# Causal attention's first batch: half of the query stores and loads, and the first maxima, sent by ScalarE

## What is computed

```
x = x + causal_attention(layernorm(x))    # 32 query heads of 16, one key and value head, ALiBi bias
x = x + ffn(layernorm(x))
x = x + window_attention(layernorm(x))
x = x + ffn(layernorm(x))
```

```
qkv    = hidden_states @ Wqkv                       # q: 32 heads x 16, k and v: 16 each
scores = einsum('bqhd,bkd->bhqk', q, k) * d**-0.5   # plus the ALiBi slope, minus 1e30 above the diagonal
probs  = softmax(scores)
attn   = einsum('bhqk,bkd->bqhd', probs, v)
out    = attn.reshape(B, S, H) @ Wo
```

## Time and profile before

| what | value |
|---|---|
| median of 3 runs | 2748.94 us |
| lowest and highest | 2740.22 and 2750.15 us |
| the profiled execution, own time | 2754.62 us |
| its span in the trace | 2752.8 us |
| its mean granted TensorE clock | 0.965 |
| first `scores` of batch 0 start at | 83.25 us |

### The profile page before, as it was taken

One profiled execution on the slowest core, in us unless ns is written; L12 is line 12 of the kernel. 1 busy time (PEld: TensorE's weight loads), 2 busy tenths in 40 slices (PEclk: granted clock), 3 DMA queues, 4 the chain that ended last, 5 costly groups with the idle time before them and its releaser, 6 DMA issues. The chain is left out here.

```text
span 2752.8 us, 41641 instructions
## 1 busy us (share of the span) xinstructions
PE 2590.5 (94%) x14444; PEld 2024.3 (74%) x14444; DVE 1731.8 (63%) x3500; ACT 1308.5 (48%) x2952; POOL 1018.4 (37%) x890
## 2 busy tenths in 40 slices
PE   4789998899999799999999998999999999799998
PEld 2445444477778588888888876888888888577777
DVE  3575656178777556565666656665666666587775
ACT  2354546332222366656666645666665666232221
POOL 2112122173333344344444423445444443443322
PEclk7889999899999999999999999999999999899999
DMA  4335242310000210011100110111001100300000
GB/s 150 111 90 139 66 114 62 85 74 1 1 0 1 64 31 16 31 38 38 38 30 8 39 39 1 39 39 38 30 8 38 38 23 1 120 1 16 16 15 16
DMA packets 113464, 117.43 MB, mean 43 GB/s; under 512 B 6244, under 2 KB 85988, under 8 KB 113316
## 3 DMA queue, kind: packets, MB, share of 16 engines
q1 hardware_dynamic: 112448, 115.51, 13.8%
q10 hardware_dynamic: 900, 0.40, 0.1%
HBM read 92.09 MB, written 22.68 MB: 42 GB/s over the span
## 5 line engine op out<-in xcount | busy, mean ns | idle before, releaser
L2024 POOL TENSOR_TENSOR rope_straight<-rope_straight,rope_crossed 128x512 f32<-128x512 f32 x160 | 207.1, 1294 | 526.8 <-DVE rope_crossed L1808 526.8
L599 POOL TENSOR_TENSOR f_hidden_low<-f_hidden,f_hidden_high 128x256 fp32r<-128x256 f32 x224 | 186.3, 852 | 427.8 <-ACT f_hidden_high L539 427.6
L1826 DVE TENSOR_TENSOR o_low<-o_sum,o_high 128x512 fp32r<-128x512 f32 x128 | 88.5, 692 | 316.5 <-ACT o_high L2004 316.2
L1035 DVE TENSOR_REDUCE a_max<-a_work 128x1 f32<-128x384 f32 (+3 forms) x352 | 205.5, 635 | 110.8 <-PE a_work L923 108.7
L1918 ACT ACTIVATE probs<-probs,exp_bias 128x256 f32<-128x256 f32 (+1 forms) x512 | 240.2, 471 | 3.3 <-DVE exp_bias L1791 3.2
L1160 ACT ACTIVATE a_probs<-a_scores 128x512 f32<-128x512 f32 x320 | 173.9, 597 | 141.2 <-PE a_scores L937 70.7
L1929 ACT CAST q_high<-rope_straight 128x512 fp32r<-128x512 f32 x128 | 79.5, 621 | 298.4 <-POOL rope_straight L2024 298.4
L1923 ACT ACTIVATE probs<-probs,exp_sum_inverse 128x256 f32<-128x256 f32 (+1 forms) x512 | 205.1, 471 | 32.4 <-DVE exp_sum_inverse L1796 32.4
L539 ACT CAST f_hidden_high<-f_hidden 128x512 fp32r<-128x512 f32 x112 | 69.5, 620 | 314.2 <-PE f_acc L296 159.8
L1628 PE MATMUL w_sum<-o_high,wo_high 128*128 128x512 f32 x512 | 204.9, 400 | 8.7 <-DVE xt L1833 4.8
L1628 PE MATMUL w_sum<-o_high,wo_low 128*128 128x512 f32 x512 | 204.2, 399 | 0.0
(11 more groups left out here) (241 smaller groups left out, 7435.9 us busy)
## 6 DMA issues: line engine op xcount, KB each, us to landing
a_queries<-a_q_stacked SPq DMA_DIRECT2D x16, 1024.0 KB, 6.1
wq_raw<-in_L_attn_b_wq SPq DMA_DIRECT2D x32, 512.0 KB, 3.7
wo_raw<-in_L_attn_b_wo SPq DMA_DIRECT2D x16, 1024.0 KB, 6.5
a_q_stacked<-a_q_part_high SPq DMA_DIRECT2D x32, 256.0 KB
f_w_raw<-in_L_ffn_w SPq DMA_DIRECT2D x14, 512.0 KB, 10.5
f_w_raw<-in_L_ffn_w2t SPq DMA_DIRECT2D x14, 512.0 KB, 11.3
a_q_stacked<-a_q_part_low SPq DMA_DIRECT2D x16, 256.0 KB
wkv_raw<-in_L_attn_b_wk SPq DMA_DIRECT2D x16, 256.0 KB, 6.5
```

The source lines that it names most:

```text
L599: e.tensor_tensor(hl[:, j % 2, cols], hm[:, cols], f32(hh[:, j % 2, cols]), ALU.subtract).then_inc(hl_ready, 1)
L1035: e.tensor_reduce(mx[:, t % 2, to:to + nh], bank, AX.X, ALU.max).then_inc(work_free[k], 1)
L2024: e.tensor_tensor(ra[:, slot], ra[:, slot], rb[:, slot], ALU.add).then_inc(roped, 1)
```

## The change

Four functions that issue DMAs move out of SyncE's program, get the engine `e` as an argument, and are called by ScalarE too. In batch 0 ScalarE now issues the query stores of m = 1 (after its cast of m = 2) and of m = 3 (after its cast of m = 3), the query loads of tiles 1 and 3 (after the squares of batch 1) and the maxima of tile 0. SyncE keeps the stores of m = 0 and 2 and the loads of tiles 0 and 2. The loads of `wo_raw` and of batch 2's `x` move behind the maxima of tile 1. Later batches are as before.

```
+        def send_queries(e, b, m):
+            if m == 0:
+                for t in range(ST):
+                    wait(e, q_landed[t], 16 * b)
+            e.wait_ge(q_low, b * DT + m + 1)
+            half, head = divmod(8 * m, HEADS)
+            for row, part in ((R_QHI, qsh), (R_QLO, qsl), (R_QHI2, qsh)):
+                to = q_dram[half, row:row + AD, head:head + 8, :].rearrange("d h t -> h d t")
+                e.dma_start(to, f32(part[:, m % 2])).then_inc(q_stored[m % 2], 16)
+
+        def load_queries(e, b, t):
+            if b:
+                e.wait_ge(scores_full, (b - 1) * UNITS_A + 4 * (t + 1) * (t + 2))
+            e.dma_start(f32(qa[:, :, t * P:(t + 1) * P]),
+                        q_dram[:, :, :, t * P:(t + 1) * P].rearrange("a r h t -> (a r) h t")).then_inc(q_landed[t], 16)
...
         @block.scalar
...
                     e.copy(qsh[:, i % 2], bank[:, :]).then_inc(q_high, 1)
+                    if b == 0 and i >= 2:
+                        e.wait_ge(q_rows_in, 32)
+                        send_queries(e, 0, 2 * i - 3)
                 elif kind == "mT":
                     e.wait_ge(full, n)
                     wait(e, m_landed[i % 2], 32 * (b * 2 + i // 2))
                     e.activation(mh[:, i % 2], bank[0:AH, 0:P], ACT.Copy, scale=-1.0).then_inc(m_high, 1)
+                    if b == 0 and i == 0:
+                        send_max(e, 0, 0)
...
                     if step == ["mean", 1, 0]:
                         for d in range(DT):
                             square(1, d)
+                        queries_stored(e, 0)
+                        e.wait_ge(masks_ready, 3)
+                        for t in (1, 3):
+                            load_queries(e, 0, t)
...
         @block.sync
...
             e.wait_ge(q_rows_in, 32)
-            for m in range(DT):
-                send_queries(0, m)
-            queries_stored(0)
+            for m in (0, 2):
+                send_queries(e, 0, m)
+            queries_stored(e, 0)
             e.wait_ge(masks_ready, 3)
-            for t in range(ST):
-                load_queries(0, t)
-            e.dma_start(wo_raw[:, :, :], wo.rearrange("(t p) n -> p t n", p=P)).then_inc(wo_in, 16)
-            send_max(0, 0)
-            load_x(2)
+            for t in (0, 2):
+                load_queries(e, 0, t)
...
                 if b == 0:
-                    send_max(0, 1)
+                    send_max(e, 0, 1)
+                    e.dma_start(wo_raw[:, :, :], wo.rearrange("(t p) n -> p t n", p=P)).then_inc(wo_in, 16)
+                    load_x(2)
```

More of the change, by code:

```diff
@@ L846, in load_last, with queries_stored, send_max @@
                     .then_inc(out_landed[m], 16)
+        def send_queries(e, b, m):
[12 more added lines that the diff above has]
+                        q_dram[:, :, :, t * P:(t + 1) * P].rearrange("a r h t -> (a r) h t")).then_inc(q_landed[t], 16)
+        def queries_stored(e, b):
+            for k in range(2):
+                e.wait_ge(q_stored[k], 48 * DT // 2 * (b + 1))
+        def send_max(e, b, t):
+            par = t % 2
+            e.wait_ge(m_low, b * ST + t + 1)
+            for row, part in ((R_MAX, mh), (R_MAX + 1, ml)):
+                e.dma_start(f32(qa[row:row + 65:64, :, t * P:(t + 1) * P]), f32(part[:, par, :])).then_inc(m_landed[par], 16)
         block = st.enter_context(nc.Block())
@@ L1303, in send_keys @@
                         e.dma_start(f32(keys[b % 2][r:r + AD, :]), f32(part[32:KV, :])).then_inc(k_landed, 16)
-            def send_queries(b, m):
-                if m == 0:
-                    for t in range(ST):
[L1308 to L1329, removed]
             def load_sums(b):
@@ L1388, in _ @@
                 if b == 0:
-                    send_max(0, 1)
+                    send_max(e, 0, 1)
+                    e.dma_start(wo_raw[:, :, :], wo.rearrange("(t p) n -> p t n", p=P)).then_inc(wo_in, 16)
+                    load_x(2)
                 if more:
-                    send_queries(b + 1, 0)
-                    send_queries(b + 1, 1)
+                    send_queries(e, b + 1, 0)
+                    send_queries(e, b + 1, 1)
                 if b:
-                    send_max(b, 2)
+                    send_max(e, b, 2)
                     store_inverses(b - 1)
@@ L1398, in _ @@
                 if more:
-                    send_queries(b + 1, 2)
+                    send_queries(e, b + 1, 2)
                 if b == 0:
-                    send_max(0, 2)
+                    send_max(e, 0, 2)
                 if more:
[L1403 to L1406, removed]
+                    send_queries(e, b + 1, 3)
+                    queries_stored(e, b + 1)
+                    load_queries(e, b + 1, 0)
+                    load_queries(e, b + 1, 1)
                 for qt in range(2):
@@ L1409, in _ @@
                         store_out(e, b, qt, half)
-                send_max(b, 3)
+                send_max(e, b, 3)
                 if b == 0:
@@ L1413, in _ @@
                 if more:
-                    load_queries(b + 1, 2)
+                    load_queries(e, b + 1, 2)
                 for half in range(2):
@@ L1417, in _ @@
                 if more:
-                    send_max(b + 1, 0)
-                    send_max(b + 1, 1)
-                    load_queries(b + 1, 3)
+                    send_max(e, b + 1, 0)
+                    send_max(e, b + 1, 1)
+                    load_queries(e, b + 1, 3)
             e.wait_ge(inv_ready, NB)
```

## The result

The changed kernel takes 2751.85 us (median of 20 runs, 2745.38 to 2760.87), the kernel before 2745.91 us in the 20 runs beside it (one of these took 6270 us; without it the median is 2745.69). The ratio is 1.0020 with a 95% interval of 1.0012 to 1.0029, which is 3.3 to 8.0 us slower. The forecast was 5.3 us slower and 2754, with 2745 to 2761 as its range.

The account below looks back on a forecast made before the run. The prediction took TensorE, busy 94% of the span, as the bound, so only its first `scores` mattered: layernorm +8.7 us, maxima ready 8.8 late, their wait -3.4, in all +5.3 on the median 2748.94, giving 2754, range 2745 to 2761.

Parts of the forecast that it names:

- What bounds the start: Before TensorE's first `scores`, the layernorm of batch 1 (70.39 us), not the load (68.57), is the last thing the maxima await.
- Stores of m = 1, +7.9 us: ScalarE issues them only behind its cast of m = 2, so its cast of m = 3 comes at 60.0, not 52.13.
- Half of the engines: Query stores use half of the DMA engines, fully; the two queues' stores share the same eight, at a share of 0.5.
- the rival of two queues beside each other: ScalarE's stores meet free DMA engines, m = 1 lands at 55.7, +1.0 us in all, 2750; chance 0.12.
- Stores of m = 3: Issued by ScalarE from 61.35 us, landed at 68.2 instead of 62.53, +5.7 us.
- ScalarE's issues ahead of the squares, +0.8 us: ScalarE issues DMAs until 63.1 though batch 1's squares could begin at 62.3, making the layernorm +8.7 us.
- ScalarE's issue of the loads: Two loads on ScalarE take 2.46 us from 68.2, end before the seed is wanted at 72.1, and cost nothing.
- The rival: The loads block ScalarE for 3.4 and 3.54 us, +3.0 on the layernorm, +8.3 in all; chance 0.14.
- Tile 0 shared with tile 1: Loads from two queues each get half the rate, so tile 0 is there at 77.8 us, level with VectorE's 79.1.
- Maxima, -3.4 us: TensorE's wait for tile 0's maxima falls from 6.1 to 2.7 us through the moves of `wo_raw` and the maxima.
- Sum: First `scores` start at 88.6 us against 83.25, +5.3 us.
- The shift reaches the end: From the first `scores` on, every engine follows TensorE, so a shift of that start passes to the end one for one.

Follow-up runs that it names:

- stores only: The kernel before with only the query stores of m = 1 and m = 3 moved to ScalarE; ratio to before 1.0024, median 2753.23 us.
- with 16 engines: The kernel before with Wqkv's query columns ordered (feature, head), so a store's slowest dimension is 16, not 8; ratios to before 0.9978 and, run again, 0.9970.
- loads only: The kernel before with only the query loads of tiles 1 and 3 moved to ScalarE; ratio to before 0.9994.
- changed, 16 engines: The changed kernel with Wqkv's query columns ordered (feature, head), slowest store dimension 16; ratios to the kernel before 0.9978 and, run again, 0.9985.
- weights behind only: The kernel before with only `wo_raw` and batch 2's `x` moved behind the maxima of tile 1; ratio to before 0.9992, median 2745.01 us.

## Why the prediction was right

*What bounds the start.* Right. In every kernel VectorE goes from the layernorm of batch 1 to its first maximum with no gap of over 0.1 us, and in "stores only" and with 16 engines TensorE is seen waiting for it.

*Stores of m = 1, +7.9 us.* It measured +6.0 (58.17 for 52.13), just below the 59 to 61 us that I gave as a sign of being right. The mechanism was right: the store stands behind a cast that waits for other stores. I let ScalarE issue at 48.9, when its cast has ended, and it issued at 47.61, which is 1.3 us less. Of these, 0.7 us are m = 0, which landed that much earlier. The rest is that the issue came 0.08 us after the cast began and not after its end; all that these stores wait for, the low part of m = 1, had been ready since 43.1. The other 0.5 us lie in the six stores themselves, 10.6 us from issue to use for 11.1. With m = 1 put back behind its own cast, the same kernel is 5.6 us faster to the `scores`.

*Half of the engines.* Shown as a share: 0.51 with one queue or two, 0.89 with a slowest dimension of 16. So the rival of two queues beside each other was out. One remark of the prediction was not quite right: SyncE was held up a little by issuing stores before, its fifth took 1.64 us (from 43.97) where the first took 0.66. Nothing waited for it.

*Stores of m = 3.* 59.56 to 66.43 is 6.9 us, the forecast's 61.35 to 68.2 as well.

*ScalarE's issues ahead of the squares, +0.8 us.* It measured 1.1: the squares start 1.84 us after VectorE's mean, 0.72 before. The layernorm came out at +7.1 (77.52 for 70.39), with 8.7 forecast.

*ScalarE's issue of the loads.* Costs nothing in the changed kernel: they end at 70.20 and the seed starts at 70.45. I had written 2.46 us for them and left 1.4 us of room; they took 3.76 and 0.25 was left. In "loads only" the cover is gone, and the seed is 2.7 us late. The rival was nearer than its 0.14 said.

*Tile 0 shared with tile 1.* 9.3 us after its issue, forecast 9.6; 6.3 in "stores only", where the four loads stand in one queue.

*Maxima, -3.4 us.* 84.29 to 87.00 is 2.7 us, as forecast, but the reason given was wrong. I put the 3.4 us down to the moves of `wo_raw` and of the maxima. "Stores only" moves neither and waits 3.1 us. The wait shrank because the maxima came 7.1 us later and the loads ahead of them only 3.9. The moves gave 0.4 us of it.

*Sum.* +3.75 us at the `scores` for +5.3. Counted from the cast it is +3.85, and two ways lead there. With the weights moved first the steps are -3.9, then +2.1 for ScalarE's issues with m = 1 early, then +5.6 for the late issue of m = 1. With the stores moved first they are +3.9, then -0.1 for all the rest. Each way adds up by construction. That they differ shows that the 3.9 us of the weights and the 5.6 us of the late issue hold only in the kernels in which they were measured.

That the medians' +5.9 lies nearer to 5.3 than the start's +3.75 does is in part luck, since the sum was 1.5 us too large at the `scores`. And the range of 2745 to 2761 holds the old median of 2748.94 too, so that the time fell into it tests little; the timeline tests the working.

*The shift reaches the end.* Right in the medians within what they can tell. Along the way it isn't constant. VectorE's reciprocal of batch 2's sums lies at 446.46 us before and at 450.21 now, +3.75, and the whole spans differ by 3.6. GpSimd's first sum of batch 2's layernorm, though, stands at 132.40 before and 139.50 now, +7.1. Between them the granted clock differs. One stretch of 18 us of the kernel before, and the one 4 us later of the changed kernel:

```profile
112.00:130.00 18.00, 16.01 (x135) 8.75 (x133) 11.56 (x23) 8.01 (x13) 2.12 (x1) 0.91 0.23 65
```
```profile
116.00:134.00 18.00, 17.06 (x113) 9.46 (x115) 9.13 (x18) 6.04 (x11) 0.00 (x0) 0.72 0.15 45
```

The later one is granted 0.72 and finishes 113 matmuls against 135. Further on the difference is given back. It doesn't belong to the late start: "stores only", whose `scores` start at 86.95, is granted 1.00 in both stretches. What makes the 2 us between the start's +3.75 and the medians' +5.9 is open. The clock is one candidate. Another is that the one profiled execution of the kernel before had a late twelfth store and so late `scores`, which would make the usual shift larger than +3.75. The interval of 3.3 to 8.0 holds both values.

## What to carry to other kernels

A DMA moved to an engine's queue goes out where that engine's program has come to, and its waits become the DMA's. Here half of the stores came to stand behind a cast that waits for the other half, which opened two holes and cost 5.6 us against the same kernel with m = 1 issued one cast earlier, while two queues moved no more than one. Before a second queue is tried, look at the DMA share: here it stood at a half with packets waiting, the shape of the transfer was what limited it, and a slowest dimension of 16 instead of 8 in all four batches gave 6 to 8 us (ratios 0.9978 and 0.9970). And put no bulk load that isn't needed soon ahead of a small one that is: in the kernel before, moving `wo_raw` (and `x`) behind the maxima took 3.9 us from the start, up to 0.9 of it perhaps by the earlier landing of the stores, though the medians are too coarse to show it. The same move gave nothing where the layernorm was late: what a wait is worth has to be read in the kernel that it will stand in.

## What the runs showed of the hardware

- DMA issues on ScalarE went out before the end of the work ahead of them: 47.61 against a cast from 47.53 to 48.12, and in "changed, 16 engines" a load goes out at 57.08, before the last square, which stands ahead of it in the program, starts at 57.43. Work behind an issue waited: the seed of "loads only" starts at 66.04, when the issue of 62.12 to 66.00 has ended.
- Two small DMAs of 16 KB landed and released TensorE 2.7 us after the first issue where nothing was ahead of them (76.94 to 79.66 in "weights behind only", 84.29 to 87.00 in the changed kernel), and 6.1 us after it with the rest of 5 MB in the queue (77.16 to 83.25, before).
- TensorE's granted clock went to half, 1.2 GHz, between 50 and 53 us in all of these kernels; full speed, 2.4 GHz, came back 3.3 to 6.3 us after the first `scores`. The kernel with 16 engines had both 6.1 and 3.3 in its two profiles, so one execution doesn't say what a kernel does to this time. Starting the `scores` after an idle time of 2.3 us instead of 5.7 brought nothing that can be seen in the changed kernel (93.0 for `scores` at 87.0, and 88.8 for 83.25).
- The mean granted clock of a whole run and its time go together: of the 20 runs of the changed kernel, the fastest three (2745.38 to 2746.16 us) have 0.967 to 0.968 and the slowest (2760.87) 0.962.
